# Attention B: the memory update as one stacked product, z written by ScalarE, and value products of 128 columns

## The reference

```
sq = sigma(q)                       # sigma(x) = elu(x) + 1
A_mem = (sq @ M) / (sum(sq * z) + EPS)
A_dot = softmax(mask(q @ k.T / sqrt(dk))) @ v
A_s = beta * A_mem + (1 - beta) * A_dot
sk = sigma(k)
V_prev = (sk @ M) / (sum(sk * z) + EPS)
M_new = M + sk.T @ (v - V_prev)
z_new = z + sum(sk)
```

## Time and profile before

| | us |
|---|---|
| median of 3 runs | 1734.57 (1734.44 to 1736.59) |
| the profiled execution | 1733.57 |
| its span, first to last instruction | 1731.8 |
| mean granted TensorE clock | 0.949 of full speed |
| PE busy | 1501.8 (87% of the span) |
| DVE busy | 1354.8 (78%) |
| POOL busy | 880.2 (51%) |
| ACT busy | 813.1 (47%) |

### The profile page before, as it was taken

The page is one execution under the profiler, slowest core; times in us unless marked ns, Lnnn a source line. Parts: engine busy times, 40 slices in busy tenths (PEclk is TensorE's granted clock), DMA queues, the critical chain, the costliest instruction groups (busy, mean ns, idle before and its releaser), DMA issues. The chain is left out here.

```text
span 1731.8 us, 46136 instructions
## 1 busy us (share of the span) xinstructions
PE 1501.8 (87%) x13668; PEld 1285.4 (74%) x13668; DVE 1354.8 (78%) x3426; ACT 813.1 (47%) x1859; POOL 880.2 (51%) x1180
## 2 busy tenths in 40 slices
PE   5999999999999999996687648888888888888887
PEld 4999898998898998995566436666666666666665
DVE  5589999999999999995345366788887877788874
ACT  1556666665665666664466523333333333333331
POOL 4365565665566665654688543333343433333331
PEclk9999999999999999998799868999999999999997
DMA  4432233322222322220444232333333333333330
GB/s 141 142 94 89 78 82 91 91 81 74 81 82 91 91 76 76 80 76 15 136 124 132 58 93 86 96 99 100 98 102 97 101 97 100 98 101 100 94 92 17
DMA packets 181694, 158.10 MB, mean 91 GB/s; under 512 B 12529, under 2 KB 163185, under 8 KB 181618
## 3 DMA queue, kind: packets, MB, share of 16 engines
q1 hardware_dynamic: 181618, 157.17, 31.3%
HBM read 113.09 MB, written 44.04 MB: 91 GB/s over the span
## 5 line engine op out<-in xcount | busy, mean ns | idle before, releaser
L587 PE MATMUL a_bank<-a_vp,a_prob 128*128 128x96 f32 x4096 | 635.2, 261 | 0.0
L587 PEld LDWEIGHTS a_bank<-a_vp,a_prob 128*128 128x128 f32 x4096 | 610.7, 192 | 5.6
L481 ACT ACTIVATE a_prob<-a_bank 128x512 f32<-128x512 f32 x512 | 305.9, 598 | 267.9 <-PE a_bank L571 267.0
L675 DVE TENSOR_REDUCE a_nmax<-a_bank 128x2 f32<-128x512 f32 x512 | 345.1, 680 | 47.7 <-PE a_bank L556 40.7
L556 PE MATMUL a_bank<-a_k_st,a_q_st 96*128 96x256 bf16 x1024 | 259.2, 276 | 36.3 <-DVE a_nmax L675 35.1
L571 PE MATMUL a_bank<-a_q_st,a_k_st 120*128 120x256 bf16 x1024 | 281.7, 276 | 3.2 <-POOL a_q_st L344 3.2
L1613 PE MATMUL c_o_bank<-c_vb,c_prob 128*128 128x96 f32 x1024 | 176.6, 297 | 30.1 <-DVE c_ad L1896 29.3
L344 POOL TENSOR_SCALAR a_q_st<-a_mt 24x2048 bf16<-24x2048 bf16 x64 | 121.4, 1896 | 138.9 <-PE a_bank L571 94.8
L1771 DVE TENSOR_REDUCE c_nmax<-c_bank 128x4 f32<-128x512 f32 x256 | 165.0, 681 | 31.4 <-PE c_bank L1583 29.9
L1487 ACT ACTIVATE c_prob<-c_bank 128x256 f32<-128x256 f32 x256 | 98.8, 386 | 176.2 <-PE c_bank L1563 174.5
L1613 PEld LDWEIGHTS c_o_bank<-c_vb,c_prob 128*128 128x128 f32 x1024 | 141.1, 199 | 41.4 <-DVE c_ad L1896 29.1
(11 more groups left out here) (202 smaller groups left out, 2999.8 us busy)
## 6 DMA issues: line engine op xcount, KB each, us to landing
a_q_st<-scratch_a_parts_dram SPq DMA_DIRECT2D x64, 288.0 KB
a_k_st<-scratch_a_parts_dram SPq DMA_DIRECT2D x192, 96.0 KB
c_q_st<-scratch_c_parts_dram SPq DMA_DIRECT2D x64, 288.0 KB
c_k_st<-scratch_c_parts_dram SPq DMA_DIRECT2D x192, 96.0 KB
scratch_a_parts_dram<-a_parts SPq DMA_DIRECT2D x32, 384.0 KB, 2.7
scratch_c_parts_dram<-c_parts SPq DMA_DIRECT2D x32, 384.0 KB, 2.7
a_x<-in_x SPq DMA_DIRECT2D x32, 128.0 KB, 3.2
scratch_y<-a_y SPq DMA_DIRECT2D x32, 128.0 KB, 2.7
```

What stands on the lines that cost most here:

```text
L481: act.activation(prob[h % 4][:, :, :].rearrange("p a b -> p (a b)"), t_ps[h % 2][:, :], ACT.Exp).then_inc(exped, 1)
L587: mm = pe.matmul(o_ps[g % 2][:, at:at + VC], prob[h % 4][:, c, t * P:(t + 1) * P], vp[o][:, c, :], start=c == 0, stop=c == NT - 1)
L675: dve.tensor_reduce(nmax[:, t, 2 * g:2 * g + 2], s_ps[t][:, :].rearrange("p (h k) -> p h k", h=2), AX.X, ALU.max, negate=True).then_inc(ma ...
```

## The change

WIN goes from 96 to 128. The lower half of skn gets the negated keys of chunks 1 and 2 by a second ScalarE operation; DVE writes the previous values (ps_c x dr) to the lower half of uv for the next chunk, so that the update product over 128 rows gives sk.T v - sk.T V_prev, and the subtraction L1808 goes. am is then made on rows 64 to 128 alone, which are the ones that the output reads, and PE waits by `read_d` until that is done. z of the next block is written by ScalarE at s = 6 as x times rs plus shift, with shift = -mean times rs made by GpSimd in two more operations.

```diff
-        WIN = 96
+        WIN = 128
+        negm, shift = sb("negm", [P, NT]), sb("shift", [P, NT])
...
                 pool.tensor_scalar(var[k][:, :], mv[k][:, :, 1], EPS, 1.0, ALU.add, ALU.mult).then_inc(norm_d[k], 1)
+                if k == 0:
+                    pool.tensor_scalar(negm[:, :], mv[0][:, :, 0], -1.0, 1.0, ALU.mult, ALU.mult
+                                       ).then_inc(norm_d[0], 1)
+                    pool.wait_ge(norm_d[0], NORM * b + 2)
+                    pool.tensor_tensor(rs[0][:, :], var[0][:, :], half[:, :], ALU.pow).then_inc(norm_d[0], 1)
+                    pool.wait_ge(norm_d[0], NORM * b + 3)
+                    pool.tensor_tensor(shift[:, :], negm[:, :], rs[0][:, :], ALU.mult).then_inc(norm_d[0], 1)
+                    return
...
                         act.copy(skn[0:SEG, :, :].rearrange("p s f -> p (s f)"),
                                  ps_c[0:SEG, 0:(NS - 1) * P]).then_inc(sk_d, 1)
+                        act.mul(skn[SEG:P, 1:NS - 1, :].rearrange("p s f -> p (s f)"),
+                                ps_c[0:SEG, P:(NS - 1) * P], -1.0).then_inc(sk_d, 1)
...
+                    if s == 6 and active(j, u, -1):
+                        act.wait_ge(norm_d[0], NORM * (n + 2))
+                        if later(j, n, 1):
+                            act.wait_ge(zt_p, n)
+                        for t in range(NT):
+                            act.activation(z[1 - i][:, t, :], x[1 - i][:, t, :], ACT.Identity,
+                                           scale=rs[0][:, t:t + 1], bias=shift[:, t:t + 1]).then_inc(z_d, 1)
...
                         if c == 0:
-                            pe.wait_ge(sk_d, b + 1)
+                            pe.wait_ge(sk_d, 2 * (b + 1))
                             pe.wait_ge(vs_d, b + 1)
                         else:
                             pe.wait_ge(u_d, b * 2 + c)
+                            pe.wait_ge(read_d, b * 9 + 3 * c)
...
                     elif k == 2:
-                        dve.tensor_tensor(by_head(am[o][:, c, :]), by_head(ps_c[:, 0:HV]),
-                                          dr[:, c, :].unsqueeze(2).broadcast_to([P, H, HD]), ALU.mult
+                        if c < 2:
+                            dve.tensor_tensor(by_head(uv[o][SEG:P, c + 1, 0:HV]),
+                                              by_head(ps_c[0:SEG, 0:HV]),
+                                              dr[0:SEG, c, :].unsqueeze(2).broadcast_to([SEG, H, HD]), ALU.mult
+                                              ).then_inc(u_d, 1)
+                        dve.tensor_tensor(by_head(am[o][SEG:P, c, :]), by_head(ps_c[SEG:P, 0:HV]),
+                                          dr[SEG:P, c, :].unsqueeze(2).broadcast_to([SEG, H, HD]), ALU.mult
                                           ).then_inc(read_d, 1)
-                    elif c < 2:
-                        dve.tensor_tensor(uv[o][0:SEG, c + 1, 0:HV], uv[o][0:SEG, c + 1, 0:HV],
-                                          am[o][0:SEG, c, :], ALU.subtract).then_inc(u_d, 1)
...
-                    if s == 7 and active(j, u, -1):
-                        if later(j, n, 1):
-                            dve.wait_ge(zt_p, n)
-                        normed(0, n + 1, x[o], z[o], z_d)
```

More of the change, by code:

```diff
@@ L1274, in attention_b @@
         flat = lambda a: a[:, :, :].rearrange("p c f -> p (c f)")
-        N_LOAD, N_LATE, SPLIT, MP, AD, VD = 3, 4, 4, 8, 6, 4
+        N_LOAD, N_LATE, SPLIT, MP, AD, VD, NORM = 3, 4, 4, 8, 6, 4, 4
         MT_AT = (3, 7)
@@ L1455, in body @@
                 if isinstance(j, int) and -1 <= n < 1:
-                    pool.wait_ge(norm_d[0], 2 * (n + 2))
+                    pool.wait_ge(norm_d[0], NORM * (n + 2))
                     value_consts(n + 1)
@@ L1827, in body @@
                         if later(j, n, 0):
-                            dve.wait_ge(norm_d[0], 2 * (n + 1))
+                            dve.wait_ge(norm_d[0], NORM * (n + 1))
                         moments(0, n + 1, x[o])
@@ L1839, in body @@
                     if s == 4 and active(j, u, 1):
-                        for k in range(4):
+                        for k in range(3):
                             read(1, k)
@@ L1845, in body @@
                             split_max(1, k)
-                            read(2, k)
+                            if k < 3:
+                                read(2, k)
                     if s == 2 and active(j, u, 1):
-                        for k in range(4):
+                        for k in range(3):
                             read(0, k)
```

## The result

The changed kernel takes 1690.2 us (median of 4 runs, 1688.16 to 1695.82) against 1734.6 us before: a ratio of 0.9747, with a 95% interval of 0.9722 to 0.9771. The profiled execution took 1689.99 us.

What follows compares the result with a forecast made beforehand. PE bounds attention B's loop, busy 88% with holes. From 1733.57 us, -45.8 for 29 iterations, +4.5 for clock falls and -2.2 for the end gave 1690.1; predicted 1690, range 1682 to 1697 at 0.68.

Steps and rivals of the forecast that it cites:

- an input in PSUM protects: DVE's new write: with one operand in PSUM like L1804, at most 0.292 us, it isn't held up by GpSimd.
- Iteration: Attention B's loop: 20.29 - 0.31 - 0.05 = 19.93 us; 29 of them 578.0 against 623.82, -45.8 us.
- Four falls: Granted clock in the 29 loop iterations: four falls left in at 1.13 us each, +4.5 us.
- The end: Last 69 us: one iteration's contention and clock, and 0.3 us in each of the others, estimated -2.2 us.
- The start: Stage start: longer norm and slower z cost some 0.7 us once, an early contended L1808 gives about as much back.
- The hole before g = 0: PE's 0.99 us wait before that value product: moving z off DVE gains 0.31 us of 0.45, ends 0 and 0.45.
- the next late thing is GpSimd's L1406: GpSimd's copy of the values ends at 1384.71, so PE starts at about 1384.75 in place of 1385.06.
- Two operations in place of one: DVE's new write and am no longer wait for each other: 0.05 us off, PE's hole 0.77 to 0.72 us.
- 128 columns: PE's L1613 records keep their pace at the new width: 0 us, with 40 us in all as upper end.
- ScalarE and GpSimd: z's two operations 0.6 to 0.96 us in 1.40 us idle; second skn copy costs nothing; shift 0.5 us early.
- the five: Rivals: clock still falls 0.12; columns cost 0.05; new write blocked 0.04; ScalarE table reloads 0.03; 0.99 us hole stays 0.05.
- Rival 1: Attention B's loop: clock still falls in every second iteration, +11 us, 1701; in all 29, 1718; chance 0.12.

Runs made afterwards that it cites:

- the pair of superfluous subtractions: Changed kernel plus one unread DVE subtraction in each of chunks 0 and 1: one input in PSUM 1716.9 us, both in SBUF 1765.6 us.
- the kernel with both orders swapped: Changed kernel with DVE's read(0) ahead of step 2's two maxima and second norm's statistics behind split and memory update: 1.0256, 1779.4 us.

## Why the prediction was right, and where its steps were not

The forecast was 1690, and 1690.2 was measured. The mechanism that carries it is shown: L1808 was blocked because both its inputs lay in SBUF (the pair of superfluous subtractions), the clock fell behind the long hole (it fell 19 times in the kernel with z alone, where the hole is in all 29 iterations, and once in the one with the stacked product alone), and the stacked product takes both away. One step towards it wasn't shown by its rows, though it came out right: the prediction read from L1804, never over 0.292 us, that an input in PSUM protects, but none of those 96 starts while L1427 runs, and only 22 while another tensor_tensor of GpSimd does, with 0.04 to 0.37 us of it left. It took the pair, and am in the changed kernel, to show it. And the last digit is owed to errors that cancel:

- **Iteration.** 19.93 us were worked out, 20.18 measured. 29 times 0.25 is 7 us too little; the stretch came out 6.3 longer than the 578.0, since its first iterations are shorter.
- **Clock.** Four falls were left in, 4.5 us; there were none.
- **The end.** -2.2 us estimated, -5.9 measured, with a clock of 0.92 in place of 0.80. The terms named (0.99 + 1.13 for one iteration, 0.3 for each of the others) add up to more than 2.2 as they stand; what they leave out is the clock of the drain.
- **The start.** Taken to net 0, it costs 1.8 us, 1.2 of them in the trace ahead of anything the change touches. So the loop came out 1.8 us longer than forecast (584.3 against 578.0 + 4.5), the end 3.7 shorter and the start 1.8 longer, -0.1 in all: that is luck.
- **The hole before g = 0.** 0.31 us was to come off it, 0.44 did. The step that failed is "the next late thing is GpSimd's L1406": PE starts at 1383.34, before GpSimd's last copy ends at 1383.44. At g = 0 PE needs the values of the block that GpSimd copied one iteration earlier; I had read the wait of the wrong block. The chain through c_ad is still what ends last.
- **Two operations in place of one.** I took 0.05 us off, from four L1896 in 1.02 us. 0.25 was a mean of two things: those four start 0.21, 0.30 and 0.21 us apart, and the 0.30 is where the rows go from 0 to 64, in all 32 iterations of the trace of before. The two operations here follow each other 0.32 us apart, and x3 another 0.32 behind. The range of 0 to 0.1 that I gave had the wrong sign: the clean iteration grew by 0.33 us with the stacked product alone, and am on 128 rows gives 0.29 back.
- **128 columns.** Taken at 0; four records take 0.03 us longer with what follows them, but the iteration only 0.05, by the kernel without them. In the time it is nothing that the runs can tell.
- **ScalarE and GpSimd.** Two z operations 0.87 us (0.6 to 0.96 given), the negated copy covered, shift early: as forecast.
- **Rivals.** None of the five came. Rival 1 can be seen in other kernels: holes of 1.01 and 1.04 us behind the step 3 value product bring a fall in every fifth or sixth iteration. The 0.75 us of the changed kernel stays below that.

The parts don't add up: alone they give -1.4, +0.3 and -0.2%, together -2.5%. z's gain needs the contention gone, and the last 32 columns help, if anywhere, in the drain.

What stays open: whether the blocking of z4 in the kernel with both orders swapped and that of the subtraction are one mechanism; what sets the drain's clock, which was seen in one trace of most kernels, two of the changed one; why a hole of 1.03 us before g = 0 brings next to no falls and one of 1.04 before the update product five; and that the kernel without the wider columns is slower at all, since the two intervals overlap.

## What to carry to other kernels

Where iterations of one loop come in two lengths, look for what differs between them before pricing any operation: here one 1.0 us block and the slow clock behind it were worth more than everything that was removed. An engine moved nearer to another's work by 0.4 us can walk into a race and lose 1 us, so test a rearrangement with the contention gone first. And where GpSimd works beside DVE, let the DVE tensor_tensor on the critical chain read one input from PSUM rather than both from SBUF.

## What the runs showed of the hardware

- DVE started x3 (rows from 0) 0.32 us behind am on rows 64 to 128 and 0.21 us behind am on all rows; behind the new write, which reads from row 0 and writes from row 64, am comes after 0.31 to 0.32 us in both. The four L1896 of before start 0.21, 0.30 and 0.21 us apart, rows from 0, 0, 64 and 64. All of these fit a loss of 0.1 us where an input's or the output's first partition changes from one operation to the next: the second then starts only after the first has ended. Doing twice the rows was the faster choice, by 0.5%.
- The granted clock falls behind short holes in a stream that is busy 87 to 90% of the time, and the length of the longest hole alone doesn't decide: none or one fall in 29 iterations with 0.56 to 0.78 us before the update product and up to 1.03 us before g = 0; every fifth or sixth iteration with 1.01 us before the value projection or 1.04 before the update product; 15 to 19 falls in 29 with 1.76 us there.
- The records of an f32 product with 128 x 128 weights follow each other after 0.112 us at 128 columns and 0.136 at 160.
- GpSimd's tensor_tensor of 128 x 512 holds up DVE's tensor_tensor with both inputs in SBUF by 0.9 to 1.0 us if it started first, and is held up itself by 0.1 to 0.16 us if DVE's did or came within 0.006 us. It held up none with an input in PSUM, in 31 starts within 0.09 us of its own in each of two kernels. Beside sg on GpSimd two tensor_scalar operations of z4 took 1.3 us longer together.
